# Sixteen-head causal attention in blocks of 64 by 64 instead of 128 by 128, with its masks added on TensorE

## The reference, cut to what matters

```
x = x + 0.5 * ffn(layernorm(x))          # 128 -> 512, two hidden layers of 512, -> 128
x = x + linear_attention(layernorm(x))
x = x + 0.5 * ffn(layernorm(x))          # the same weights
x = x + 0.5 * experts(layernorm(x))      # top 2 of 8
x = x + attn(layernorm(x))               # the changed one:
    q, k = rope(x Wq), rope(x Wk); v = x Wv          # 16 heads of 8 features
    scores = q k^T / sqrt(8), -inf above the diagonal # 256 x 256 per head and sequence
    out = softmax(scores) v, then Wo
x = x + 0.5 * experts(layernorm(x))
```

## Time and profile before

| | |
|---|---|
| profiled execution, its time and its span | 650.77 us, 649.0 us |
| granted TensorE clock, mean | 0.989 |
| PE busy | 620.6 us (96%), 5327 matmuls |
| PEld busy | 471.8 us (73%) |
| DVE busy | 487.9 us (75%), 1262 instructions |
| ACT busy | 485.7 us (75%), 816 |
| POOL busy | 287.1 us (44%), 443 |
| DMA | 37.79 MB, mean 58 GB/s |

### The profile page before, as it was taken

The page is one execution under the profiler, slowest core; times in us unless marked ns, Lnnn a source line. Parts: engine busy times, 40 slices in busy tenths (PEclk is TensorE's granted clock), DMA queues, the critical chain, the costliest instruction groups (busy, mean ns, idle before and its releaser), DMA issues.

```text
span 649.0 us, 14237 instructions
## 1 busy us (share of the span) xinstructions
PE 620.6 (96%) x5327; PEld 471.8 (73%) x5327; DVE 487.9 (75%) x1262; ACT 485.7 (75%) x816; POOL 287.1 (44%) x443
## 2 busy tenths in 40 slices
PE   4899999999999999999999999988999999999997
PEld 3777878888887887888778887756556666666675
DVE  6767566675766777665878767799998989989755
ACT  5789778787788787887888777624776668777882
POOL 1402303311311525223638354577787656656553
PEclk9899999999999999999999999999998989999999
DMA  9300000000000001100002025454354232231012
GB/s 292 107 2 1 0 1 2 1 2 1 1 1 2 0 2 49 49 1 1 1 26 66 8 82 163 155 175 139 103 150 144 72 103 91 68 112 53 4 36 67
DMA packets 41885, 37.79 MB, mean 58 GB/s; under 512 B 2940, under 2 KB 37020, under 8 KB 41816
## 3 DMA queue, kind: packets, MB, share of 16 engines
q1 hardware_dynamic: 41816, 36.87, 18.3%
HBM read 21.92 MB, written 14.68 MB: 56 GB/s over the span
## 4 chain that ended last, share of the span: by engine, by line
PE 70%; DVE 13%; ACT 9%; issue 6%; POOL 1%; DMA 0%; POOLq 0%; DVEq 0%; ACTq 0%
PE PSA L1015 20%; PE PSA L1019 19%; PE PSA L1252 7%; DVE MX L1439 5%; PE PSA L1228 3%; DVE G L1317 3%; PE PSA L1034 2%; PE PSA L1194 2%; ACT PSA L1486 2%; PE PSA L1171 2%; PE PSA L1178 2%; ACT G L1482 1%; PE PSA L1201 1%; PE PSA L1212 1%; PE PSA L1275 1%
## 5 line engine op out<-in xcount | busy, mean ns | idle before, releaser
L1015 PE MATMUL PSA<-ah,WH 128*128 128x512 f32 x320 | 130.0, 406 | 0.5 <-DVE G L1317 0.5
L1439 DVE TENSOR_REDUCE MX<-PSA 128x6 f32<-128x768 f32 x128 | 118.7, 951 | 13.5 <-PE PSA L1201 12.2
L1486 ACT ACTIVATE PSA<-PSA,SC 128x512 f32<-128x512 f32 x128 | 84.7, 662 | 55.0 <-PE PSA L1019 54.4
L1019 PE MATMUL PSA<-al,WH 128*128 128x512 f32 x320 | 125.2, 391 | 0.0
L1578 ACT ACTIVATE PB<-PSA 128x768 f32<-128x768 f32 x128 | 99.6, 812 | 30.8 <-PE PSA L1228 22.9
L1015 PE MATMUL PSA<-bh,WH 128*128 128x512 f32 x256 | 105.2, 411 | 2.7 <-DVE G L1317 2.3
L1019 PE MATMUL PSA<-bl,WH 128*128 128x512 f32 x256 | 100.2, 392 | 0.0
L1608 POOL TENSOR_SCALAR VE<-MV 128x4 f32<-128x4 f32 x46 | 11.4, 248 | 197.0 <-DVE MV L1292 197.0
L1322 DVE TENSOR_TENSOR al<-PSA,ah 128x512 fp32r<-128x512 f32 x64 | 44.0, 688 | 52.0 <-ACT ah L1493 51.6
L1668 POOL TENSOR_SCALAR_AFFINE_SELECT PB<-PB 128x512 f32<-128x512 f32 x95 | 60.4, 636 | 48.1 <-ACT PB L1578 46.4
L1322 DVE TENSOR_TENSOR bl<-PSA,bh 128x512 fp32r<-128x512 f32 x64 | 43.9, 687 | 34.8 <-ACT bh L1493 34.5
(11 more groups left out here) (165 smaller groups left out, 1302.2 us busy)
## 6 DMA issues: line engine op xcount, KB each, us to landing
KS<-dk SPq DMA_DIRECT2D x32, 192.0 KB
QS<-dq SPq DMA_DIRECT2D x32, 192.0 KB
dk<-CB SPq DMA_DIRECT2D x16, 192.0 KB, 2.3
dq<-CB SPq DMA_DIRECT2D x16, 192.0 KB, 2.5
VA<-in_ones SPq DMA_DIRECT2D x5, 512.0 KB, 5.1
X<-in_x SPq DMA_DIRECT2D x8, 256.0 KB, 6.8
dk<-CB SPq DMA_DIRECT2D x16, 128.0 KB, 2.1
dq<-CB SPq DMA_DIRECT2D x16, 128.0 KB, 1.9
```

Of the source, the lines that this page charges most:

```text
L1015: e.matmul(o, WH[:, col:col + 128], hi, start=first, stop=False)
L1019: return e.matmul(o, WH[:, col:col + 128], low, start=False, stop=last)
L1439: e.tensor_reduce(MX[:, u % 2, 1:4, :].rearrange("p t (l g) -> p l t g", l=2)[:, :, :, g], PSA[:, b:b + 2, 0:384].rearrange("p l (t k) -> ...
L1486: e.activation(bank(b), bank(b), ACT.Gelu, scale=SC[:, k:k + 1]).then_inc(a_gelu, 1)
```

## The change

Every 256 by 256 score matrix is now cut in blocks of 64. Of the 16 blocks of a head the 10 on and below the diagonal are computed, and two heads are stored in 640 columns instead of 768.

- `pass1`: 12 matmuls on 64 by 64 quarters of the array instead of 8 on halves. One 64-wide diagonal mask (L1194 before, L1192 after), then scores with 64, 128, 256 and 192 columns (L1199). The row half `h` still has a PSUM bank of its own. The maximum is taken over five blocks of 64 (640 columns). One of the five belongs to a different query block on each half of the partitions, so `peak` becomes one reduction and two additions with a cap of -3e38 (`CAP`).
- `pass2`: 12 matmuls on quarters instead of 4 or 8. Masks are always added by TensorE (L1227), and GpSimd's select is gone. The two row halves `l` write to the same bank, on different halves of the partitions.
- The exponential covers 640 columns. `weighed` has two steps per sequence of 16 matmuls (256, 64, 192 and 128 columns in each of four strips) instead of four steps of 8.
- `value` writes 64 by 64 blocks; `vexp` is two instructions for 64 partitions each; the maxima's halves are transposed by a matmul into fp32 (L1215) and copied from there.
- The template with the ones is copied by GpSimd (`ones`, five copies of 1024 columns from `TPL`) instead of loaded by DMA; the constant rows shrink to two per half and come in two DMAs per lot of buffers (`rows`), before the `reloc`s.
- Order: `attend` has priority 1 instead of 2.5, `opening` 1 instead of 4, and the `pass1` jobs of the first three sequences 1.5 instead of 5.5 or 6.5. `QUEUED` is 2.0 until both streams are done. `SHIFT` and the costs in `TAKES` are new throughout.

```diff
-TILES = {"pass1": "h", "pass2": "h", "weigh": "q", "weighed": "q", "max_out": "q"}
+TILES = {"pass1": "h", "pass2": "h", "weighed": "q", "max_out": "q", "value": "c"}
...
-QUEUED = 1.0
+QUEUED = (2.0, 1.0)
+FIRST = (3, 1.5)
...
-    ("after", 0, 0): 0.67, ("after", 0, 2): -0.08, ("after", 0, 5): -0.22, ("after", 0, 6): 0.4,
...
+    ("after", 0, 2): -0.16, ("after", 0, 6): -0.02, ("after", 1, 7): 0.49, ("attend", 0): -0.02,
...
-                if self.clock[eng] < self.clock["P"] + QUEUED and self.bank[b] is not None and self.bank[b + 1] is not None and self.left(self.bank[b] + self.bank[b + 1]) <= self.clock["P"] + AHEAD:
+                if self.clock[eng] < self.clock["P"] + QUEUED[len(self.dead) > 1] and self.bank[b] is not None and self.bank[b + 1] is not None and self.left(self.bank[b] + self.bank[b + 1]) <= self.clock["P"] + AHEAD:
...
-            self.add(2.5, self.attend(2 * c + h, a, va), of=("attend", 2 * c + h))
+            self.add(1, self.attend(2 * c + h, a, va), of=("attend", 2 * c + h))
...
-        for n in range(KEPT):
+        for m, lot in ((1, LOTS[0]), (2, LOTS[1])):
             while len(self.dead) < m:
                 yield
             yield from self.until(self.dead[m - 1].done)
             if m == 2:
                 self.sr.ids = [6, 7, 5, 4]
+            self.put("rows", i=m - 1, x=m, src=self.dead[m - 1])
+            for n in lot:
+                self.qfree[n] = [self.dead[m - 1]]
+            while self.turn["reloc"] <= lot[-1]:
+                yield
+            for n in lot:
+                self.vfree[n] = [self.put("ones", i=n, x=m, src=self.dead[m - 1])]
...
-        self.add(self.lead, self.peaks(u, rl), "h", ("peaks", u))
+        self.add(FIRST[1] if u < FIRST[0] else self.lead, self.peaks(u, rl), "h", ("peaks", u))
...
+        for g in range(2):
+            while len(ps) < 4 * g + 4:
                 yield
+            yield from self.until(ps[4 * g + 3].done)
+            while self.otfree[u % 2] is None:
+                yield
+            b, free = yield from self.sr.get(self)
+            w = self.put("weighed", u=u, g=g, b=b, emptied=free, emptied2=self.otfree[u % 2])
...
                 elif st.name == "pass1":
                     K, Q = KS[u % KEPT], QS[u % KEPT]
                     w.wait_ge(s_qs[u % KEPT], 64 * (u // KEPT + 1))
...
+                    w.wait_ge(s_far[u % KEPT in LOTS[1]], 32)
+                    w.wait_ge(g_c, 5)
+                    emptied(w, st.emptied)
+                    for x in range(2):
                         for h in range(2):
...
+                            o = PSA[64 * x:64 * x + 64, b + h, 128:384] if x else PSA[0:64, b + h, 192:320]
+                            e.matmul(o.rearrange("p (t k) -> p t k", t=2)[:, :, 0:64], IM[64 * h:64 * h + 64, 0, 0:64],
+                                     MK[64 * h:64 * h + 64, 0, :, 0:64], start=True, stop=False, skip_group_check=True)
+
+                    for q, at in (((0, 1), (256, 192)), ((3, 2), (0, 0))):
+                        for x in range(2):
+                            for h in range(2):
+                                m = 64 * q[x] + 64
+                                t = e.matmul(PSA[64 * x:64 * x + 64, b + h, at[x]:at[x] + m], Q[64 * h:64 * h + 48, g, m - 64:m],
+                                             K[64 * h:64 * h + 48, g, 0:m], start=False, stop=True, skip_group_check=True)
                     t.then_inc(p_pass1, 1)
...
                 elif st.name == "pass2":
                     K, Q = KS[u % KEPT], QS[u % KEPT]
                     w.wait_ge(s_m[u % KEPT], 32 * (u // KEPT + 1))
                     emptied(w, st.emptied)
...
+                    part = lambda x, l: (slice(64 * (l ^ x), 64 * (l ^ x) + 64), b + x)
+                    for x in range(2):
+                        for l in range(2):
+                            R, k = part(x, l)
+                            o = PSA[R, k, 0:384] if x else PSA[R, k, 0:512]
+                            e.matmul(o.rearrange("p (t q) -> p t q", t=2)[:, :, 0:64], MK[64 * l:64 * l + 64, 0, 0, 0:64],
+                                     IM[64 * l:64 * l + 64, 0, 0:64].rearrange("p (o q) -> p o q", o=1).to_broadcast([64, 2, 64]),
+                                     start=True, stop=False, skip_group_check=True)
+
+                    for js in ((0, 1), (3, 2)):
+                        for x in range(2):
+                            for l in range(2):
+                                R, k = part(x, l)
+                                j, at = js[x], (256, 192)[x] * (js[0] == 3)
+                                t = e.matmul(PSA[R, k, at:at + 256 - 64 * j], K[64 * l:64 * l + 50, g, 64 * j:64 * j + 64],
+                                             Q[64 * l:64 * l + 50, g, 64 * j:256], start=False, stop=True, skip_group_check=True)
+                    t.then_inc(p_pass2, 1)
+                elif st.name == "weighed":
+
+                    V = VA[u % KEPT]
+                    w.wait_ge(a_prob, 8 * u + 4 * g + 4)
+                    w.wait_ge(a_vexp, u + 1)
+                    emptied(w, st.emptied)
+                    for k, j in enumerate((0, 3, 1, 2)):
+                        at = (0, 256, 0, 192)[k]
+                        for v in range(4):
+                            t = e.matmul(PSA[32 * v:32 * v + 32, b, 64 * j:256], V[:, 8 * (k % 2) + 4 * g + v, k // 2, :],
+                                         PB[:, 4 * g + v, k // 2, at:at + 256 - 64 * j], start=(k == 0), stop=(k == 3),
                                          skip_group_check=True)
...
                     t.then_inc(p_weigh, 1)
...
                 elif st.name == "pass1":
                     w.wait_ge(p_pass1, n + 1)
-                    e.tensor_reduce(MX[:, u % 2, 1:4, :].rearrange("p t (l g) -> p l t g", l=2)[:, :, :, g],
-                                    PSA[:, b:b + 2, 0:384].rearrange("p l (t k) -> p l t k", t=3), AX,
+                    e.tensor_reduce(MX[:, u % 2, :, :].rearrange("p t (l g) -> p l t g", l=2)[:, :, :, g],
+                                    PSA[:, b:b + 2, 0:320].rearrange("p l (t k) -> p l t k", t=5), AX,
                                     ALU.max).then_inc(v_mx, 1)
                 elif st.name == "peak":
                     w.wait_ge(v_mx, st.src.n + 1)
-                    w.wait_ge(g_c, 3)
+                    w.wait_ge(v_cap, 4)
                     w.wait_ge(g_hm, n - 1)
-                    e.tensor_reduce(PK[:, u % 2, :, :], MX[:, u % 2, :, :].rearrange("p (q k) h -> p q h k", k=2), AX,
-                                    ALU.max).then_inc(v_peak, 1)
+                    M = MX[:, u % 2, :, :]
+                    e.tensor_reduce(PK[:, u % 2, 1, :], M[:, 0:3, :].rearrange("p k h -> p h k"), AX, ALU.max).then_inc(
+                        v_peak, 1)
+
+                    e.scalar_tensor_tensor(out=PK[:, u % 2, 0, :], in0=M[:, 3, :], scalar=CAP[:, 0:1], in1=M[:, 4, :],
+                                           op0=ALU.add, op1=ALU.max)
+                    w.wait_ge(v_peak, 2 * n + 1)
+                    e.scalar_tensor_tensor(out=PK[:, u % 2, 1, :], in0=M[:, 3, :], scalar=CAP[:, 1:2],
+                                           in1=PK[:, u % 2, 1, :], op0=ALU.add, op1=ALU.max).then_inc(v_peak, 1)
                 elif st.name == "max_out":
                     w.wait_ge(p_max, n + 1)
                     if u >= 2:
                         w.wait_ge(s_m[(u - 2) % KEPT], 32 * ((u - 2) // KEPT + 1))
-                    e.tensor_copy(MT[:, u % 2, :], PSA[0:32, b, 0:128].bitcast(BF16)).then_inc(v_mt, 1)
+                    e.tensor_copy(MT[:, u % 2, :], PSA[0:32, b, 0:256]).then_inc(v_mt, 1)
...
-                    e.activation(PB[:, n % SLOTS, :, :, :].rearrange("p t l q -> p l t q"),
-                                 PSA[:, b:b + 2, 0:384].rearrange("p l (t q) -> p l t q", t=3), ACT.Exp,
-                                 scale=SCALE).then_inc(a_prob, 1)
+                        w.wait_ge(p_weigh, 2 * s.u + s.g + 1)
+                    e.activation(PB[:, g, :, :], PSA[:, b:b + 2, 0:320], ACT.Exp, scale=SCALE).then_inc(a_prob, 1)
...
+                elif st.name == "ones":
+
+                    ffns_dead(w, st.x)
+                    w.wait_ge(s_rest, n_w4)
+                    e.tensor_copy(VA[i][:, :, :, :].rearrange("p s a r -> p s (a r)"), TPL[:, :, :].rearrange(
+                        "p (o a) r -> p o (a r)", o=1).to_broadcast([128, 16, 64])).then_inc(g_one, 1)
...
-                elif st.name == "pass2" and st.kind != "m":
-                    P = PB[:, n % SLOTS, 0:2, :, :].rearrange("p t l q -> p (t l) q")
-                    w.wait_ge(a_prob, n + 1)
-                    e.affine_select(out=P, in_=P, compare_op=ALU.is_ge, fill=0.0, base=0,
-                                    pattern=[[0, 4], [1, 128]], channel_multiplier=-1).then_inc(g_sel, 1)
...
-                elif st.name == "ones":
+                elif st.name == "rows":
 
                     ffns_dead(w, st.x)
```

(10 more changed lines are left out.)

208 lines of the change are left out of this document (78 added, 130 removed), and 10 rows, old and new, of the table TAKES.

## The result

The changed kernel took 642.85 us (median of 4 runs, 639.3 to 645.81), the kernel before 648.65 us beside it (4 runs); the ratio is 0.991, interval 0.9885 to 0.9935. A second measurement, 643.14 us (6 runs), gave 0.9891 (0.9857 to 0.9924). That is 5.8 us faster (7.0 by the second), where the prediction had 17. 642.85 lies outside the forecast's own range (625 to 638) and at the very top of the one that takes in the rivals (620 to 643); the nearest value on record is the rival "waits eat it" (639.5). The profiled execution took 645.81 us, its span 644.0, at a mean granted clock of 0.984.

What follows compares the result with a forecast made beforehand. VectorE was taken to pace 412 to 617 us, TensorE a close second. -12.4 (VectorE), -3 (early first passes) and -2 (end) make -17.4 from 650.8, 633.4; the runs' median lies 2.4 lower, so 631 us, range 625 to 638.

Steps and rivals of the forecast that it cites:

- waits eat it: Rival: in the web of three engines only ScalarE's net 7.1 us at its 80% share counts, 639.5 us; chance 0.15.
- I take VectorE as what paces 412 to 617 us: Between first and last maximum VectorE, about 90% busy, sets the pace, with TensorE a close second.
- At a 90% share of the stage this shortens it by 11.2/0.90 = 12.4 us: VectorE's net saving of 11.2 us, divided by its busy share, shortens the stage by 12.4 us.
- The amount of work saved: VectorE's net busy time over the whole change: 11.2 us less, from 10 to 12.4.
- TensorE as the close second: In the 412 to 617 us stage TensorE saves 23.3 us, at least 16, and stays behind VectorE as a bound.
- The rival at 624: Rival: TensorE was the bound after all, so its whole 23.3 us are gained, 624 us; chance 0.13.
- The early first passes: Earlier first operands fill 3 of VectorE's 4.6 free us from 393 to 412 us: -3 us (0 to 5).
- The warned-of sign: The prediction is wrong if the feed-forward streams end later than 428 us by more than they gain.
- The clock, left as it was: Slow-clock stretches from 460 to 540 us, 5.2 us of TensorE, stay unchanged; 3 us allowed either way.
- Prices per instruction: Maximum 816 ns, exponential near 705 ns; `peak` +4.8 us and the `MT` copy +1.2 us in all on VectorE.
- The two slow rivals: Passes slow to 0.41 us: row halves take turns in second passes, 651 us (0.07), or column halves in both, 677 us (0.05).
- The end, -2 us: After the last maximum, the last 32 us: two sequences' shorter exponentials (1.7 us) and the select save 2 us.

Runs made afterwards that it cites:

- b_max107: Kernel before, same order, each maximum over 642 instead of 768 columns, to relieve VectorE alone: 646.04 us, ratio 0.9959.
- b_nomask1: Kernel before, same order, without the four mask matmuls of each first pass, to relieve TensorE alone: 648.05 us, ratio 0.9985.
- a_mtfirst: Changed kernel with SyncE's order alone altered, reloads of sequences 3 and 4 behind the send of the first maxima: 641.56 us, ratio 0.9891.
- b_noselect: Kernel before, same order, without GpSimd's 95 selects (those diagonal blocks stay unmasked): 646.72 us, ratio 0.9985.

## Why the prediction was wrong

- **What bounds the kernel: wrong.** The failed step is "I take VectorE as what paces 412 to 617 us", and with it "At a 90% share of the stage this shortens it by 11.2/0.90 = 12.4 us". In the profiled executions the last maximum came only 4.6 us earlier (612.1 for 616.7). 16.6 us taken off VectorE alone bought 2.7 us (b_max107), about a sixth; TensorE, ScalarE and GpSimd alone bought at most 1 us each, all four together 12.7. What the runs show in its place: in this fixed order no engine's sum paces the stage, and savings on several engines count together where single ones hardly count. That it is the waits between them that do this is the reading, not a measurement. The argument for that step was that TensorE's 97% (96.2 by its own rows) "hides slack" and VectorE's 90% little. But of TensorE's 200.06 us between 412 and 620 only 11.42 are fillers; without them it is at 188.6 of 208 us, 91%, no less than VectorE's 90%, so the shares could not tell the two apart. The same stage, fillers alone (length, PE, PEld, clock, DMA):

```profile
412.00:620.00 208.00, 11.42 (x120) 7.35 (x120) 0.98 0.32 101
```

  The amount of work saved is not what failed: 11.9 us for a forecast of 11.2, though only by luck that near, since the touched items gave 7.4.
- **TensorE as the close second: no better.** 14.8 us off TensorE alone bought 1 us (b_nomask1, not to be told from 0; 2.7 at equal clock), 13.6 in the changed kernel at most 2. The rival at 624 is refuted, though TensorE's own parts came as forecast: 0.20 to 0.22 us for a pass, 1.22 for a weighing.
- **"Waits eat it", 639.5 us, was the nearest**, though its sum (ScalarE's saving over its share) is refuted too: ScalarE alone bought nothing. That it came nearest is therefore in part luck; what holds is its first sentence, the web. The savings on several engines are worth more together (12.7 us against 5.1), and the change relieves all four: it gives 5 to 9 us without tables, and 9 at full clock.
- **The early first passes, -3 us: wrong.** Worth 0.3 us on these blocks and -4.1 on the old ones. The warned-of sign came: the last of the streams was 4.6 us late, while the first exponential gained 1.2 us of the 12 foreseen. From 412 to 430 us VectorE was busy for 17.01 of 18 us (before 16.29), with seven maxima (5.5 us) where five (4.6 us) had stood; TensorE was busy for 17.60 (17.14). Which of the two held the streams up is not shown.
- **The order was taken as given.** Neither the sum nor a rival had a term for how well the table of offsets fits its order. It is worth 11 to 12 us in each kernel; one that belongs to another order leaves a kernel 16 us behind its own. The two tables happened to be worth nearly the same, so this didn't move the result, but it could have moved it by more than any term of the sum.
- **The clock, left as it was: wrong, by about 3 us.** Low clock doubled, from 3.2 to 6.2 us on average. That is just the 3 us that the prediction allowed for it.
- **Prices per instruction: right for the maximum and the exponential**, with `peak` and `MT` 4.2 us dearer. **The two slow rivals: refuted** by 0.20 to 0.22 us per pass.
- **The end, -2 us:** the last maximum to the end of the span was 31.9 us, before 32.3. The saving is hardly to be seen.

What stays open: how the 9 us at full clock divide among the four engines in the changed kernel, since the parts don't add; and whether another table, or an order planned for one engine's saving alone, would give more. No version of the whole computation that was tried beats the changed kernel clearly: 641.56 us (a_mtfirst) has the same ratio.

## What to carry to other kernels

Where two engines stand near 90% in a stage with a fixed order, don't divide one engine's saving by its share. Ask first what the stage does when one engine alone is relieved, by cutting its columns: here a sixth of the saving came back, and two to two and a half times the sum of the parts when all were cut. And where an order was tuned by a table, compare a change both with and without the table before a price is put on any part of it.

## What the runs showed of the hardware

- Four 64-by-64 quarters of the array run beside each other, with 8 + 4 matmuls in 0.20 to 0.22 us, also with two row halves writing to different partitions of one PSUM bank.
- TensorE's granted clock fell to 1.2 GHz for 7 and 13 us in a stage where it was busy for 93% of the time, with gaps of less than a microsecond in what the records show. Kernels with less TensorE work and the same order had more of it: 7.1 us low instead of 3.4 (first-pass masks left out before), 11.8 instead of 6.2 (all masks left out after). The order matters too: the kernel before with early first passes has nearly the same matmuls (46 fillers and 4 masks more), and 8.1 us low beside 2.9. More fillers raised the clock little (4.8 us low instead of 6.2) and cost more than they gave.
- Some of VectorE's operations from SBUF to SBUF took less time in the runs where GpSimd had less to do. The normalisation on VectorE has a median of 340 ns in both kernels, but its mean fell from 394 (27.0 us in all, 78 of them) to 366 ns:

```profile
L1306 DVE TENSOR_SCALAR XN<-X,MV,RS 128x128 f32<-128x128 f32 x78 | 25.0, 366 | 0.0
```

  With the selects alone gone (b_noselect) its mean was 382 ns and VectorE's busy time fell by 2.5 us, from 487.9 to 485.4, with the same instructions. That the two engines hold each other up is a guess; no run isolates it. Against a general rule: single normalisations of up to 1181 ns stand in that trace too, and another group from SBUF to SBUF (`al` from `G` and `ah`, 64 of them) took 0.7 us more in the changed kernel, not less. It is a gain in busy time that no term of the prediction had; how much of it reached the time is not shown.
- An operation of 16 columns with two operands takes 240 to 275 ns on VectorE, more than a 48-column reduction (196 ns).
